# Layer 1 of a twelve-layer kernel: the turns, copies and lifts of its attention in another order, and its values placed by GpSimd

## The reference, cut to what matters

```python
def _L0_xattn_ref(hidden_states, ssm_states, Wq, Wk, Wv, Wsk, Wsv, Wo):
    ...
    q = _heads(jnp.concatenate([ssm_states, hidden_states], axis=-1) @ Wq, H)
    k = _heads(hidden_states @ Wk, HK)
    v = _heads(hidden_states @ Wv, HK)
    ssm_k = _heads(ssm_states @ Wsk, HK)
    ssm_v = _heads(ssm_states @ Wsv, HK)
    ...
    o = _attend(q, kcat, vcat)
    o = o.transpose(0, 2, 1, 3).reshape(B, T, HID)
    return o @ Wo
```

```python
x = _layernorm(x + _L0_xattn_ref(x, ctx_2048, L0_xattn_Wq, ...), axis=-1)
x = _layernorm(x + _L0_ffn_ref(x, L0_ffn_weight, ...), axis=-1)
```

## Time and profile before

| | us |
|---|---|
| median of 3 runs | 2064.90 |
| the runs | 2047.86, 2064.90, 2065.36 |
| the profiled execution, its own time | 2067.79 |
| its span in the profile | 2065.7 |

### The profile page before, as it was taken

One profiled execution on the slowest core, in us unless ns is written; L12 is line 12 of the kernel. 1 busy time (PEld: TensorE's weight loads), 2 busy tenths in 40 slices (PEclk: granted clock), 3 DMA queues, 4 the chain that ended last, 5 costly groups with the idle time before them and its releaser, 6 DMA issues.

```text
span 2065.7 us, 29988 instructions
## 1 busy us (share of the span) xinstructions
PE 1865.6 (90%) x11144; PEld 1444.2 (70%) x11144; DVE 1266.4 (61%) x2731; ACT 1012.4 (49%) x2253; POOL 618.2 (30%) x654
## 2 busy tenths in 40 slices
PE   8998998999999798799999989858999788999796
PEld 6885777788878544588888856637888544555685
DVE  4555766567777845554444454784444567888566
ACT  3214766355555577233333314644333378988232
POOL 1212100233332411122222224442222245888212
PEclk9998877999999989799999999878999898999798
DMA  5005400301011100133332300010232001000011
GB/s 216 27 26 122 74 1 19 118 1 41 2 39 39 39 1 2 45 100 105 109 134 92 117 11 1 1 39 33 100 130 83 31 0 39 1 1 1 0 62 41
DMA packets 25620, 105.55 MB, mean 51 GB/s; under 512 B 3642, under 2 KB 9530, under 8 KB 21508
## 3 DMA queue, kind: packets, MB, share of 16 engines
q1 hardware_dynamic: 23316, 101.87, 14.5%
q0 software_dynamic: 1728, 1.58, 0.6%
q10 hardware_dynamic: 432, 0.20, 0.0%
HBM read 97.56 MB, written 6.07 MB: 50 GB/s over the span
## 4 chain that ended last, share of the span: by engine, by line
PE 71%; DVE 11%; ACT 9%; issue 3%; POOL 2%; DMA 2%; SPq 0%; POOLq 0%; DVEq 0%; ACTq 0%
PE ps L145 64%; PE ps L262 7%; ACT AR L148 3%; DVE AR L162 2%; DVE AR L151 2%; DVE Y L151 1%; POOL AR L151 1%; DVE stt L329 1%; ACT CR L148 1%; DVE AR L159 1%; DMA AR<-sq 1%; DVE X L156 1%; ACT AR L1921 1%; DVE CR L162 1%; POOL R L151 1%
## 5 line engine op out<-in xcount | busy, mean ns | idle before, releaser
L145 PE MATMUL ps<-R 128*128 128x512 f32 (+3 forms) x4944 | 881.1, 343 | 44.0 <-DVE R L151 14.5
L145 PEld LDWEIGHTS ps<-R 128*128 128x128 f32 (+1 forms) x4944 | 747.2, 194 | 161.8 <-issue 15.8
L151 POOL TENSOR_TENSOR R<-W,R 128x768 fp32r<-128x768 f32 (+2 forms) x106 | 181.5, 1719 | 614.0 <-ACT R L2187 497.6
L148 ACT ACTIVATE AR<-AR 128x512 f32<-128x512 f32 (+2 forms) x584 | 276.8, 546 | 154.9 <-DVE AR L162 108.0
L151 DVE TENSOR_TENSOR AR<-ps,AR 128x512 f32<-128x512 f32 (+5 forms) x266 | 137.4, 536 | 235.7 <-PE ps L145 214.7
L2213 ACT CAST R<-AR 128x512 fp32r<-128x512 f32 x148 | 92.0, 621 | 303.7 <-DVE AR L151 294.0
L145 PE MATMUL ps<-W,AR 128*128 128x256 f32 (+3 forms) x1184 | 209.6, 364 | 9.8 <-ACT AR L1504 9.3
L262 PEld LDWEIGHTS ps<-cf,AR 128*128 128x128 f32 (+5 forms) x904 | 115.6, 148 | 125.7 <-issue 62.2
L262 PE MATMUL ps<-cf,AR 128*128 128x128 f32 (+5 forms) x904 | 154.5, 290 | 38.2 <-POOL AR L151 14.2
L145 PEld LDWEIGHTS ps<-W,AR 128*128 128x128 f32 (+2 forms) x1184 | 157.5, 170 | 41.5 <-issue 17.6
L165 DVE TENSOR_TENSOR_SCAN AR<-AR,ps 128x512 f32<-128x512 f32 x128 | 154.2, 1216 | 33.1 <-PE ps L262 24.0
(11 more groups left out here) (203 smaller groups left out, 2163.6 us busy)
## 6 DMA issues: line engine op xcount, KB each, us to landing
W<-in_wts SPq DMA_DIRECT2D x14, 1920.0 KB, 8.5
AR<-shd SPq DMA_DIRECT2D x32, 512.0 KB, 3.6
W<-in_wts SPq DMA_DIRECT2D x4, 2048.0 KB, 8.4
AR<-shd SPq DMA_DIRECT2D x20, 384.0 KB, 3.4
W<-in_wts SPq DMA_DIRECT2D x5, 1280.0 KB, 7.5
AR<-shd SPq DMA_DIRECT2D x20, 256.0 KB, 3.9
W<-in_wts SPq DMA_DIRECT2D x2, 1536.0 KB, 7.8
AR<-shd SPq DMA_DIRECT2D x20, 128.0 KB, 3.6
```

The lines of the kernel that those rows point to most:

```text
L145: return self.e.matmul(o, l, r, start=start, stop=stop, skip_group_check=True)
L148: return self.e.activation(o, i, f, bias=bias, scale=scale)
L151: return self.e.tensor_tensor(o, a, b, op)
```

## The change

Six things, in layer 1 and where layers 2 and 3 join it:

- PE's turns are single steps now, `turn(j)`. Round v turns step 2v-3 before the values, and step 2v-2 last. Each waits for the copy that frees its own bank.
- ACT's list alternates: exponential 2v, copy 2v-3, exponential 2v+1, copy 2v-2. The copy of `oturn`'s result stands before copy 2v-3 at t4 = 2.
- The two lifts of a sequence are counted one by one and stand a round apart: the first at the end of ACT's round with t4 = 3, the second at the end of the next (t4 = 0).
- PE's end-of-sequence steps stand right behind the scores: first half at t4 = 0, second at 1, `oturn` at 2, `out` at 3. `state` and `vals` stand behind the values.
- The 11 copies that place the values, and the ones, go from DVE to GpSimd, each waiting for the one before it.
- Behind the last round ACT's work is put in a new order: lifts of sequence 7 first, then layer 3's lambda and splits, then `lora.act_exp`. `out(6)` and `pe_logits(5)` come before `upright(7, 0)` on PE.

DVE's list is unchanged but for what it loses. The diff, cut to its core (the counts of `vplaced` and `lifted` change with it, 24 to 8 and 8 to 16):

```diff
@@ -839,8 +838,8 @@
                     b, t = divmod(u, 4)
                     O = banks[(5, 1)[b % 2]]
                     e.wait_ge(*T.copied.at(2 * u + 2))
-                    e.wait_ge(*T.vplaced.at(3 * b + 3))
-                    e.wait_ge(*T.lifted.at(b - 1))
+                    e.wait_ge(*T.vplaced.at(b + 1))
+                    e.wait_ge(*T.lifted.at(2 * b - 2))
...
+                def turn(j):
+
+                    if not 0 <= j < 64:
+                        return
+                    e.wait_ge(*T.copied.at(j - 1))
+                    e.wait_ge(*T.low.at(7))
+                    e.wait_ge(*T.exped.at(j + 1))
+                    pe_turn(e, self.E[j % 4], banks[(4, 6)[j % 2]]).then_inc(T.turned.sem, 1)
...
-                    e.wait_ge(*T.lifted.at(b + 1))
+                    e.wait_ge(*T.lifted.at(2 * b + hf + 1))
...
                         scores(v)
                     if 2 <= v < 6:
                         last_third(v - 2)
+                    if t4 == 0 and B >= 2:
+                        upright(B - 2, 0)
+                    if t4 == 1 and B >= 2:
+                        upright(B - 2, 1)
+                    if t4 == 2 and B >= 2:
+                        oturn(B - 2)
+                    if t4 == 3 and B >= 2:
+                        out(B - 2)
+                    turn(2 * v - 3)
+                    if 0 <= v - 3 < 32:
+                        values(v - 3)
+                    if t4 == 1 and B >= 3:
+                        state(B - 3)
                     if t4 == 3 and B < 7:
                         vals(B + 1)
-                    if 0 <= v - 3 < 32:
-                        values(v - 3)
-                    if 0 <= v - 1 < 32:
-                        e.wait_ge(*T.copied.at(2 * v - 2))
-                        e.wait_ge(*T.low.at(7))
-                        for x in range(2):
-                            j = 2 * v - 2 + x
-                            e.wait_ge(*T.exped.at(j + 1))
-                            pe_turn(e, self.E[j % 4], banks[(4, 6)[x]]).then_inc(T.turned.sem, 1)
-                    if t4 == 3 and B >= 1:
-                        upright(B - 1, 0)
-                    if t4 == 0 and B >= 2:
-                        upright(B - 2, 1)
-                    if t4 == 1 and B >= 2:
-                        oturn(B - 2)
-                    if t4 == 2 and B >= 2:
-                        out(B - 2)
+                    turn(2 * v - 2)
                     if v == 32:
                         for b in range(5):
                             lora.pe_logits(e, b)
-                    if t4 == 1 and B >= 3:
-                        state(B - 3)
 
                 lora.pe_rank(e, 0)
+                out(6)
+                lora.pe_logits(e, 5)
                 upright(7, 0)
                 lora.pe_rank(e, 1)
-                lora.pe_logits(e, 5)
...
-                for x in range(2):
-                    e.wait_ge(*T.zeroed.at(x + 1))
-                    for _, _, n, c, p0, j in VPIECES:
-                        e.e.memset(self.vp(x)[p0:p0 + n, :, c, j, 8:9], 1.0).then_inc(e.sem, e.up())
-
-                def place_values(b, pieces):
-                    e.settle()
-                    e.wait_ge(*T.vcopied.at(b + 1))
-                    e.wait_ge(*T.valued.at(4 * (b - 1)))
-                    for src, r0, n, c, p0, j in VPIECES[pieces]:
-                        t = e.e.tensor_copy(self.vp(b)[p0:p0 + n, :, c, j, 0:8],
-                                            self.VT[b % 2][r0:r0 + n, 64 * src:64 * src + 64].rearrange("p (g d) -> p g d", g=8))
-                    t.then_inc(T.vplaced.sem, 1)
...
-                    if i == 1:
-                        for x in range(3):
-                            place_values(0, self.PIECES[x])
-                    if i % 8 in (1, 3, 5) and i > 8:
-                        place_values(i // 8, self.PIECES[i % 8 // 2])
...
+                def exp(i):
+                    E, m = self.E[i % 4], self.m[i % 4]
+                    e.wait_ge(*T.maxed.at(i + 1))
...
+                    t.then_inc(T.exped.sem, 1)
+                def copy(j):
+                    e.wait_ge(*T.turned.at(j + 1))
+                    e.wait_ge(*T.valued.at(j // 2 - 1))
+                    e.e.copy(self.P[j % 4], banks[(4, 6)[j % 2]]).then_inc(T.copied.sem, 1)
+                def lift(b, hf):
+                    e.wait_ge(*T.valued.at(4 * b + 4))
+                    e.wait_ge(*T.upright.at(2 * b - 3 + hf))
+                    e.wait_ge(s_b[1], 96)
+                    r = slice(64 * hf, 64 * hf + 36)
+                    e.e.copy(self.OU[b % 2][r, :], banks[(5, 1)[b % 2]][r, :]).then_inc(T.lifted.sem, 1)
+                def ocopy(b):
+                    e.wait_ge(*T.oturned.at(b + 1))
+                    e.wait_ge(*T.wout.at(b))
...
+                for v in range(32):
                     B, t4 = divmod(v, 4)
...
+                    exp(2 * v)
+                    if t4 == 2 and B >= 2:
+                        ocopy(B - 2)
+                    if v >= 2:
+                        copy(2 * v - 3)
+                    exp(2 * v + 1)
+                    if v >= 1:
+                        copy(2 * v - 2)
...
-                        e.wait_ge(*T.vplaced.at(3 * (b - 1)))
+                        e.wait_ge(*T.vplaced.at(b - 1))
...
+                    if t4 == 3 and B >= 1:
+                        lift(B - 1, 0)
+                    if t4 == 0 and B >= 2:
+                        lift(B - 2, 1)
+                    if t4 == 1 and B >= 3:
                         act_copy_state(e, l, B - 3)
...
+                lora, diff = layers[2], layers[3]
+                copy(61)
+                copy(62)
+                lift(6, 1)
+                copy(63)
+                act_copy_state(e, l, 5)
+                ocopy(6)
+                lift(7, 0)
+                lift(7, 1)
+                diff.act_lambda(e)
+                for i in range(3):
+                    diff.act_split(e, 0, i)
+                lora.act_exp(e, 0)
+                lora.act_turned(e, 0)
+                lora.act_turned(e, 1)
+                ocopy(7)
...
-                for x in self.VP:
-                    e.e.memset(x, 0.0).then_inc(T.zeroed.sem, 1)
+                for x in range(2):
+                    e.e.memset(self.VP[x], 0.0).then_inc(T.zeroed.sem, 1)
                 self.bring_k(e, 0)
-                for p, s in ((0, 1), (1, 0), (1, 1), (2, 0), (2, 1)):
+                e.wait_ge(*T.zeroed.at(2))
+                for x in range(2):
+                    for _, _, n, c, p0, j in VPIECES:
+                        e.e.memset(self.vp(x)[p0:p0 + n, :, c, j, 8:9], 1.0).then_inc(e.sem, e.up())
+                        e.settle()
+
+                def queries(p, s):
                     if p and s == 0:
                         self.bring_k(e, p)
                     e.wait_ge(s_q[2 * p + s], 64)
                     e.e.tensor_copy(*self.place_q(p, s)).then_inc(T.qplaced.sem, 1)
-                for b in range(6):
+
+                def values(b):
...
+                        e.settle()
+                        t = e.e.tensor_copy(self.vp(b)[p0:p0 + n, :, c, j, 0:8],
+                                            self.VT[b % 2][r0:r0 + n, 64 * src:64 * src + 64].rearrange("p (g d) -> p g d", g=8))
+                        if i < len(VPIECES) - 1:
+                            t.then_inc(e.sem, e.up())
+                    t.then_inc(T.vplaced.sem, 1)
+                    e.wait_ge(*T.vplaced.at(b + 1))
+
+                queries(0, 1)
+                values(0)
+                queries(1, 0)
+                queries(1, 1)
+                values(1)
+                values(2)
+                queries(2, 0)
+                queries(2, 1)
+                for b in range(5):
                     pool_rstd(e, l, b)
+                    values(b + 3)
+                pool_rstd(e, l, 5)
                 e.wait_ge(*T.scored.at(32))
                 for i in range(3):
```

More of the change, by code:

```diff
@@ new lines, in act @@
+                copy(62)
[12 more added lines that the diff above has]
+                ocopy(7)
+                act_copy_state(e, l, 6)
@@ L1174, in pool @@
+                for b in range(2):
+                    lora.act_turned(e, b + 2)
+                    act_copy_state(e, 2, b)
+                    diff.X.act_block(e, b)
+                act_copy_state(e, l, 7)
+                lora.act_turned(e, 4)
+                act_copy_state(e, 2, 2)
+                diff.X.act_block(e, 2)
             def pool(self, e):
```

61 lines of the change are left out of this document (10 added, 51 removed).

## The result

The changed kernel takes 2071.1 us (median of 20 runs, 2064.0 to 2081.2), the kernel before, run beside it, 2056.8 (20 runs, 2044.5 to 2079.4). The ratio is 1.0054, 95% interval 1.0031 to 1.0077: 11 us slower, within 6 and 16. The medians stand 14.3 us apart: before's runs fall into two groups here, 11 from 2044.5 to 2057.0 and 9 from 2064.6 to 2079.4, and a median between two groups moves easily, so the ratio is the safer figure. All 20 runs of the changed kernel, 2064.0 to 2081.2, lie where before's slower group does. The profiled execution of the changed kernel took 2066.55 us (span 2064.5). That of before, 2067.79, turns out to belong to the slower group, so the two profiles have to be compared stretch by stretch.

The account below looks back on a forecast made before the run. PE's own work, much of it at the lower clock, was taken as the bound, with 2.06 us of stalls per 23.7 us sequence. Terms 2 + 1.5 - 1.2 - 2.1 + 2.5 = +2.7 on 2064.9 gave about 2068, range 2044 to 2090.

Parts of the forecast that it names:

- four signs of being wrong: No lift wait at PE's L862, steady clock above 0.85 or below 0.6, GpSimd's copies delaying `values`, a shorter layer end.
- The lift's wait: Steady part: stalls of 2.5 us a sequence against 2.06 before, +2 us over 4.3 sequences (-6 to +9).
- The chain from lift to lift: Within a sequence, first lift to second: 5.8 us at 2.4 GHz, with PE standing 2.6 us at the second `upright`.
- The baseline: Steady part: PE's 21.64 us busy a sequence and 42% of time at 2.4 GHz kept; start from median 2064.9.
- The pairs before that: From 220.5 to 251.0, one and a half sequences before the steady part: +1.5 us (-2.5 to +2.7).
- The values' placing: At the start, DVE loses memsets (-0.7 us) and copies (-1.4), GpSimd's work stays hidden: -2.1 us (0 to -5).
- The layer's end: Behind the last round, exponential, shares and addition of sequence 6 come later: +2.5 us (-1 to +5).
- allowance of -1.7: At the layer's end, PE's other waits before the last values: bounded by 2 us either way, counted as -1.7.
- The collision: GpSimd instructions and VectorE ones with two SBUF inputs exclude each other: at most a few tenths of a us a sequence.
- (C): The order does little, lift waits equal the old copy waits, start and end cancel: 2065; chance 0.54 together with the forecast.
- (A): Stalls go and the steady clock stays at 1.00: about 2046, or 2037 if lifts don't bind; chance 0.25.
- (B): Longer stalls make the steady clock fall more, 27 us a sequence: about 2083; chance 0.21.

Follow-up runs that it names:

- e3: The kernel before with only the values' placing (ones and copies) moved from DVE to GpSimd, using the changed kernel's GpSimd list: ratio 1.0023 to before.
- e2: The kernel before with layer 3's lambda, splits and `lora.act_exp` put behind the lifts of sequence 7 on ScalarE: ratio 1.0049 to before.
- e1: The changed kernel with `lora.act_exp` moved before the two lifts of sequence 7 on ScalarE: median 2067.1 us, ratio 1.0052 to before.
- e5: The changed kernel with each lift moved before the second exponential of its ScalarE round: median 2034.8 us, ratio 0.9865 to before.
- k3: The changed kernel with each lift moved later, behind the first exponential of the next round: ratio 1.0207 to before.
- before_again: The kernel before, unedited, profiled once more: steady part 80.4 us at a clock of 0.81.
- e4: The changed kernel with PE's two `upright` of a sequence moved behind turn(2v-3) and values(v-3): median 2048.0 us, ratio 0.9964 to before.
- g1: The changed kernel with the edits of e4 and e1 together: median 2040.9 us, ratio 0.9897 to before.
- g2: g1 with layer 3's lambda and splits also moved, between `lora.act_exp` and the lifts of sequence 7: 2042.1 us, ratio 0.9901 to before.
- k2: The changed kernel with the edits of e5 and e1, and GpSimd's root of sequence 6 before layer 3's subtractions: 2032.4 us, ratio 0.9860 to before.
- after_again: The changed kernel, unedited, profiled once more: steady part 89.8 us at a clock of 0.79, end 65.4 us.

## Why the prediction was right or wrong

The forecast, 2068, is 3 us under the measured median, and "the same", within 1%, came true. The nearness of the 3 us is luck. The median that it starts from, 2064.9 of three runs, stood 8.1 us above that of 20 runs, and the change was +11 by the ratio (+14 by the medians) where the sum said +2.7. The mechanism was in the main foreseen: the waits that go, the wait for the lift that comes and the later exponential are all there, and none of the four signs of being wrong appeared (PE does wait for the lifts, the steady clock is 0.79, no value is late, the end is longer). The terms were less good than the total.

- **The lift's wait.** "The two new stalls, about 1.7 and 2.6 us" are 1.83 and 2.70 where the clock stays up. The chain from lift to lift was right in place, order and size. The step that failed comes next: I took the stalls as 2.5 us a sequence, on the assumption that 43% of them meet the low clock, where both together shrink to 0.7 (and the weight of one half gives 2.45, not 2.3). In the profile no sequence was at 1.2 GHz as a whole. Before each first wait the clock was at 1.00, so it never shrank; where the clock fell behind it, the second shrank to 1.18 to 1.34, so that such a sequence still stalls for 3.1 us. The eight waits are 13.7 us, 3.4 for each of their four sequences. PE's busy time, which I kept at 21.64 us, was 75.83 / 3.75 = 20.2, at 0.79 instead of 0.71. The two errors cancel, and against the one profile of before that was known the steady part came out at +0.5 for a forecast of +2.
- **The baseline.** "I keep ... the clock's share", read from one execution. Its steady part, 89.1 us, had 80.4 and 78.3 as companions with the same code. Against those the changed order, which gave 89.6, 89.8 and 93.1, loses 9 to 15 us there. I set the profiled execution 2.9 us above the median; against 20 runs it was 11 above. Together with the end this is the main part of the difference between +2.7 and +11, as far as four profiles of before's order can tell.
- **The pairs before that.** +1.5 forecast. From step 16 to step 32 it was 47.3 and 47.7 against 42.6, 42.9 and 40.1: +4 to +8. The lift's wait stands here too (1.83 us at 240.92), and the clock was 0.78 in the third stretch instead of 0.84.
- **The values' placing.** -2.1 forecast at the start, -1.2 until 220.5. Step 2 starts 1.5 us sooner. The first scores came at 176.13, 0.6 us later than before, held by the key's DMA for 1.63 us, and the first bias at 177.05 instead of 177.15: the 0.7 us of the memsets were not won. GpSimd did the ones in 3.59 us and the 11 copies in 3.2, hidden as forecast. But step 16 starts 5.4 us sooner, with a clock of 0.79 and 0.96 in the first two stretches instead of 0.72 and 0.86, and e3 has that too, with the placing moved and nothing else changed. The gain that came with the clock was not foreseen.
- **The layer's end.** +2.5 forecast, +9.8 measured; e2 has it alone, e1 takes most of it back. The exponential was to start at 374.3 and started at 375.6, as the lifts of sequence 7, which wait for the last values, started 1.6 us later (372.74 against 371.15). Of the allowance of -1.7 nothing came. And three things were left out behind the exponential: the shares' multiplications run beside GpSimd's subtractions (2.23 us instead of 1.29); PE, without work for 4.68 us, resumes at 1.2 GHz; and all of layer 2 hangs on that.
- **The collision.** The rule of the Trainium skill ("SBUF — State Buffer", on the shared port pair), which I let pass as a few tenths since "no row here shows a collision", is met in the trace: two multiplications with both inputs in SBUF last 0.43 us alone and 2.23 beside GpSimd's subtractions, three of some 1.26 us each. Taken singly, each ends 0.05 us behind one of them: 377.35 behind 377.29, and 378.57 behind 378.51. The profile of before had it already, in DVE's and GpSimd's timelines, which I had not read against each other there:

```profile
370.33 1.29 DVE L151 TENSOR_TENSOR CR<-CR 128x40 f32<-128x40 f32 x2
```
```profile
367.57 3.75 POOL L151 TENSOR_TENSOR R<-W,R 128x512 fp32r<-128x512 f32 x3 [9.57 <-ACT R L1479]
```

The page says of the one that comes second that it "fully blocks"; the trace agrees, by these ends.

- **The rivals.** (C), that the order does little, is nearest of the three in total (2065), but start and end don't cancel as it has them. (A) is what the order does once most of the lift's wait is removed (e5: 17.5 us a sequence at 0.95 and a median of 2034.8; I had 18 for PE's work and small gaps, and 2037). (B)'s 27 us a sequence is passed by k3 with 29.4, but in another way: there the waits are 7.6 us a sequence at a clock of 0.69, where (B) had them shrink to 0.7 at a clock of 0.6. What I didn't see is that (A) was one move of the lift away.

The parts add up thus, changed kernel against before and before_again: to step 16 -5.4 and -4.4 us, to step 32 +4.7 and +4.4, steady +0.5 and +9.2, end +9.8 and +8.3, together +9.6 and +17.5 (layer 2's last state copy comes at 419.1, and at 409.5 and 401.6 in the two); the rest of the program, with the same code in all fourteen profiles, takes from 1643.6 to 1662.7 us from one execution to the next, and hides this in any single pair of profiles.

Left open: why before's order, with 6.7 to 8.2 us of waits in the steady part, had a clock of 0.70 to 0.83, while e4's order with 6.9 us, in eight waits too, held 0.93 to 0.95 in three profiles (e4, g1, g2). The sum of the waits alone doesn't settle the clock. What the rows add is what PE did before it fell. Two windows of 3 us, each behind a turn's wait for the copies, in before and in before_again:

```profile
294.50:297.50 3.00, 2.99 (x14) 2.71 (x14) 2.63 (x13) 2.16 (x8) 0.00 (x0) 0.50 0.03 8
284.90:287.90 3.00, 3.00 (x34) 2.67 (x36) 2.92 (x14) 2.45 (x10) 0.00 (x0) 0.91 0.00 0
```

In the first, `upright` had waited 1.01 us for the division 3.3 us before the turn waited 1.05; in the second, the turn alone had waited, 1.23. In the steady parts of the four profiles of before's order the first pattern comes eleven times (the turn's wait is 0.73 to 1.05 us), with the clock at 0.50 behind it each time, and the turn's wait of some 1.22 us alone five times, with 0.80 to 1.00. Whether the pair of waits brings the clock down, or both come from how a sequence meets the clock, no run here settles.

## What to carry to other kernels

When a wait is removed by moving a reader a round later, look at once for the reader that has been moved to the front of its round: the producer at the end of the other engine's round is what it will wait for, and moving the producer ahead of an operation that idles anyway can cost next to nothing (here it won some 36 us of 2071, for a move of four lines). Take a second profile of the baseline before its clock enters a sum: an engine whose clock swings needs a range, not a value. In a tail where one engine's list is reordered, follow the smallest instruction on it (0.23 us here) to whoever waits for it.

## What the runs showed of the hardware

- The same list of PE gave a steady part of 78.3, 80.4 and 89.1 us in different executions (91.5 with the values' placing moved to GpSimd, on the chip that gave 78.3), at a mean granted clock of 0.83, 0.81, 0.71 and 0.70, while the orders with longer or with shorter waits repeated themselves more closely (89.6, 89.8, 93.1; 69.5, 69.5, 71.1).
- Beside GpSimd's SBUF-to-SBUF subtractions VectorE's multiplications with two SBUF inputs last until a subtraction ends (two of them 2.23 us instead of 0.43), and so do scalings with one tensor from SBUF (1.35 us instead of 0.41 in k2, 1.17 instead of 0.17 in g2), while an addition that reads PSUM, in the midst of them at 346.79 in k2, keeps its 0.41.
- GpSimd's small instructions, each waiting for the one before: a memset of 32x8 takes 0.16 us (3.59 / 22), a copy of 32x64 0.29 (3.2 / 11), against 0.12 and 0.20 on VectorE, which does them in a row without such waits.
- Behind a wait of PE for a lift the granted clock of the next 3 us was 0.50 for each of the eight waits of 3.50 to 3.64 us in k3's steady part, 0.50 behind 2.70 in three profiles (changed, after_again, e1), and 0.80 to 1.00 behind the eight of 1.5 us in e4 and g1. Behind the four of 1.83 in the changed kernel it was 0.62 to 1.00.
